# Sparse expert layer on one core: layer two in one PSUM group with one z operation, last scaling on VectorE, weight halves in a tile per chunk, no engine loop

## What is computed

```python
# x: (4096, 128) after the first layer norm; E = 8 experts, F = 512
router_probs = softmax(x @ Wr + br)
gates = max(router_probs); idx = argmax(router_probs)
xn = (x - mean) * rsqrt(var + 1e-5) * ln_g + ln_b
h = relu(xn @ W1[idx] + b1[idx])        # layer one
y = (h @ W2[idx] + b2[idx]) * gates     # layer two
out = layernorm(x + y)
```

## Time and profile before

| | |
|---|---|
| median of 3 runs | 221.95 us (221.65 to 223.75) |
| span of the profiled execution | 219.4 us |
| PE busy | 151.0 us (69%) |
| DVE busy | 171.0 us (78%) |
| ACT busy | 141.9 us (65%) |
| POOL busy | 122.4 us (56%) |

### The profile page before, as it was taken

One profiled execution on the slowest core, in us unless ns is written; L12 is line 12 of the kernel. 1 busy time (PEld: TensorE's weight loads), 2 busy tenths in 40 slices (PEclk: granted clock), 3 DMA queues, 4 the chain that ended last, 5 costly groups with the idle time before them and its releaser, 6 DMA issues.

```text
span 219.4 us, 5683 instructions
## 1 busy us (share of the span) xinstructions
PE 151.0 (69%) x1395; PEld 125.6 (57%) x1396; DVE 171.0 (78%) x792; ACT 141.9 (65%) x425; POOL 122.4 (56%) x210
## 2 busy tenths in 40 slices
PE   0158975989785989662500199979979979979600
PEld 0014854776664768552400089869869869868500
DVE  2538789878889889986779139989979979989910
ACT  2455619473817386658502288979979979989530
POOL 4322233325728676687777220667767767768670
PEclk9999997585968596655555559999999999999955
DMA  5996760000101010100133211222221221220000
GB/s 154 334 366 190 224 185 0 3 1 0 51 0 38 17 37 14 51 25 25 37 93 106 75 37 28 65 62 56 71 73 52 64 73 54 70 62 23 30 9 0
DMA packets 16409, 15.66 MB, mean 71 GB/s; under 512 B 2810, under 2 KB 13142, under 8 KB 16386
## 3 DMA queue, kind: packets, MB, share of 16 engines
q1 hardware_dynamic: 13458, 10.83, 17.4%
q0 software_dynamic: 2272, 4.27, 5.9%
q10 hardware_dynamic: 656, 0.30, 0.5%
HBM read 10.52 MB, written 5.33 MB: 72 GB/s over the span
## 4 chain that ended last, share of the span: by engine, by line
PE 37%; POOL 18%; issue 13%; DVE 12%; ACT 8%; DMA 5%; DVEq 2%; SPq 1%; ACTq 1%; POOLq 1%
POOL rows L374 12%; PE bank L559 7%; PE bank L545 4%; PE bank L547 4%; PE bank L549 4%; PE bank L548 4%; PE bank L562 3%; PE bank L450 3%; DMA XN<-in_attn_embeddings 3%; PE bank L471 3%; PE bank L518 2%; POOL rstd L362 2%; POOL R L366 2%; ACT sq L578 2%; DVE hl L1006 2%
## 5 line engine op out<-in xcount | busy, mean ns | idle before, releaser
L405 POOL DMA_INDIRECT out<-OUT,tok x39 | 40.5, 1038 | 29.3 <-issue 29.0
L374 POOL DMA_INDIRECT rows<-R,place x32 | 33.9, 1061 | 9.0 <-issue 9.0
L545 PE MATMUL bank<-sel,bias 96*128 (+1 forms) x156 | 35.2, 225 | 5.2 <-issue 5.2
L547 PE MATMUL bank<-xh,W1h 128*128 128x128 f16 x156 | 35.0, 225 | 0.0
L549 PE MATMUL bank<-xh,W1l 128*128 128x128 f16 x156 | 34.8, 223 | 0.0
L548 PE MATMUL bank<-xl,W1h 128*128 128x128 f16 x156 | 34.7, 222 | 0.0
L559 PE MATMUL bank<-W2hl,hh 128*128 x156 | 32.7, 274 | 0.9 <-DVE hl L1006 0.8
L1006 DVE SCALAR_TENSOR_TENSOR hl<-bank,hh 128x512 f16<-128x512 f32 x39 | 26.6, 682 | 6.5 <-ACT hh L682 6.4
L450 PEld LDWEIGHTS bank<-V,C 128*128 128x128 f32 x128 | 24.9, 299 | 11.2 <-issue 11.2
L450 PE MATMUL bank<-V,C 128*128 128x129 f32 x128 | 26.8, 393 | 3.0 <-DVE Y L772 3.0
L562 PE MATMUL bank<-W2hl,hl 128*128 x156 | 28.0, 219 | 0.0
(11 more groups left out here) (162 smaller groups left out, 448.8 us busy)
## 6 DMA issues: line engine op xcount, KB each, us to landing
XR<-rows SPq DMA_DIRECT2D x39, 66.0 KB, 1.8
W<-in_ffn_W SPq DMA_DIRECT2D x1, 2048.0 KB, 11.5
X<-in_attn_embeddings SPq DMA_DIRECT2D x2, 512.0 KB, 9.0
X<-in_attn_embeddings SPq DMA_DIRECT2D x1, 768.0 KB
out<-OUT,tok POOLq DMA_INDIRECT x39, 2.3
XN<-in_attn_embeddings SPq DMA_DIRECT2D x2, 256.0 KB, 8.3
rows<-R,place POOLq DMA_INDIRECT x32, 2.4
C<-in_constants SPq DMA_DIRECT2D x1, 428.0 KB, 4.6
```

What stands on the lines that cost most here:

```text
L374: pool.indirect_dma_start(out=rows[:, :], out_offset=bass.IndirectOffsetOnAxis(ap=place[u % 4][:, k:k + 1], axis=0), in_=R[u % 4][:, k, :] ...
L405: pool.indirect_dma_start(out=out[:, :], out_offset=bass.IndirectOffsetOnAxis(ap=tok[k][:, 0:1], axis=0), in_=OUT[k][:, :], in_offset=None ...
L545: pe.matmul(h, bias3[:, c * P:(c + 1) * P], sel, start=True, stop=False)
L547: pe.matmul(h, wh, xh[k][:, :], start=False, stop=False)
```

## The change

1. Layer two: the weight halves lie in separate tiles, and all products go to the same 128 columns. Per block there are 13 products of 128 columns in place of 4 of 256 and 5 of 128: the same number of columns, four more instructions with four more weight loads. One `z` operation on DVE takes the place of `z0` and `z`.
2. The last scaling moves: `fin` is now a `tensor_scalar` on DVE (subtract the mean, multiply by rec), and `shift` is gone. ACT has no `fin`. `sd` on ACT goes from lead -2 to lead -1, and `fin` on DVE has lead -2.
3. The weight halves are cut by chunks of 128 hidden units, over all experts, in place of pairs of experts; each operation has as many elements as before.
4. There is no engine loop: all 39 blocks are written out. PE and SP load the registers for the next 8 blocks in the middle of the 8 before.

```diff
-            steps(pe, [(1, b_h), (4, b_xT), (0, b_y)], load_experts)
+            def b_next(count, k):
+                if k == UN // 2 and (count(0) + 1) * UN < NB:
+                    load_experts((count(0) + 1) * UN)
...
-                for c in range(FC):
-                    w = W2hl[:, bass.ds(e * FC + c, 1), :]
-                    pe.matmul(y[:, 0:2 * D], hh[k][:, c * P:(c + 1) * P], w, start=c == 0, stop=False)
...
+                pe.matmul(y[:, 0:D], sel16[:, count(0) * UN + k:count(0) * UN + k + 1].to_broadcast([96, P]), bias3[:, FF:FF + D], start=True, stop=False)
                 for c in range(FC):
+                    wh, wl = W2h[c][:, bass.ds(e, 1), :], W2l[c][:, bass.ds(e, 1), :]
+                    pe.matmul(y[:, 0:D], hh[k][:, c * P:(c + 1) * P], wh, start=False, stop=False)
+                    pe.matmul(y[:, 0:D], hl[k][:, c * P:(c + 1) * P], wh, start=False, stop=False)
+                    m = pe.matmul(y[:, 0:D], hh[k][:, c * P:(c + 1) * P], wl, start=False, stop=c == FC - 1)
                 m.then_inc(every["y_ps"], 1)
...
+            steps([(1, b_h), (4, b_xT), (0, b_next), (0, b_y)])
...
-            steps(act, [(5, b_xs), (1, b_hh), (-3, b_fin), (4, b_xt), (-2, b_sd), (4, b_xh)])
+            steps([(5, b_xs), (1, b_hh), (4, b_xt), (-1, b_sd), (4, b_xh)])
...
-            def b_shift(count, k):
+            def b_fin(count, k):
+                after(dve, stored[k], count(0) * 16)
                 dve.wait_ge(every["rec"], blocks(count(0), k))
...
+                ts(OUT[k][:, :], z[k][:, :], mv2[k][:, 0:1], sd[k][:, 1:2], ALU.subtract, ALU.mult).then_inc(every["out"], 1)
...
-            steps(dve, [(1, b_hl), (-1, b_mv), (0, b_z0), (-2, b_rec), (0, b_z), (-2, b_shift), (0, b_bn), (4, b_xl)])
+            steps([(1, b_hl), (-1, b_mv), (-2, b_rec), (0, b_z), (-2, b_fin), (0, b_bn), (4, b_xl)])
```

More of the change, by code:

```diff
@@ L180, in build @@
         mv2 = [sb(f"mv2{i}", [P, 2]) for i in range(UN)]
-        sd = [sb(f"sd{i}", [P, 3]) for i in range(UN)]
+        sd = [sb(f"sd{i}", [P, 2]) for i in range(UN)]
         OUT = [sb(f"OUT{i}", [P, D]) for i in range(UN)]
@@ L193, in build @@
         padded = sem("padded")
-        names2 = "xs xh xl hl z".split()
+        names2 = "xs xh xl hl".split()
         t = {n: [sem(f"b_{n}{i}") for i in range(UN)] for n in names2}
-        every = {n: sem("every_" + n) for n in "token xT_ps xt h_ps hh y_ps z0 bn mv sd rec shift out".split()}
+        every = {n: sem("every_" + n) for n in "token xT_ps xt h_ps hh y_ps z bn mv sd rec out".split()}
         seen = sem("seen")
@@ L222, in build @@
         LO_AT = (7, 9)
-        AHEAD = 1
         def after(eng, signal, count):
@@ L228, in after, with steps @@
                 eng.wait_ge(signal, count)
-        def steps(eng, stages, turn_starts=None):
+        def steps(stages):
             hi = max(lead for lead, _ in stages)
             lo = min(lead for lead, _ in stages)
[L235 to L257, removed]
+            for b in range(-hi, NB - lo):
+                for lead, f in stages:
+                    if 0 <= b + lead < NB:
+                        f(lambda d, turn=(b + lead) // UN: turn + d, (b + lead) % UN)
         def blocks(turn, k):
@@ L309, in _ @@
                 sp.wait_ge(scattered[i], 16 * NT * (NU // 4))
-            held_row = [sp.alloc_register(f"row{i}") for i in range(UN)]
+            held_row = [sp.alloc_register(f"row{i}") for i in range(2 * UN)]
             row = {}
             def load_rows(first):
-                n = min(UN, NB - first) if isinstance(first, int) else UN
-                sp.load(held_row[0:n], blk_row[0:1, bass.ds(first, n)])
+                n, half = min(UN, NB - first), first // UN % 2 * UN
+                sp.load(held_row[half:half + n], blk_row[0:1, first:first + n])
                 for j in range(n):
-                    row[j] = sp.snap(held_row[j], min_val=0, max_val=PADROW)
+                    row[first + j] = sp.snap(held_row[half + j], min_val=0, max_val=PADROW)
             def load(count, k):
-                after(sp, every["z0"], blocks(count(-1), k))
+                after(sp, every["z"], blocks(count(-1), k))
                 after(sp, every["token"], blocks(count(-1), k))
-                sp.dma_start(XR[k][:, :], rows[bass.ds(row[k], P), :]).then_inc(row_loaded[k], 16)
-            steps(sp, [(0, load)], load_rows)
+                sp.dma_start(XR[k][:, :], rows[bass.ds(row[count(0) * UN + k], P), :]).then_inc(row_loaded[k], 16)
+            load_rows(0)
+            for b in range(NB):
+                if b % UN == UN // 2 and b + UN // 2 < NB:
+                    load_rows(b + UN // 2)
+                load(lambda d, turn=b // UN: turn + d, b % UN)
             for k in range(UN):
@@ L407, in store @@
                     in_=OUT[k][:, :], in_offset=None, bounds_check=T - 1, oob_is_err=False).then_inc(stored[k], 16)
-            steps(pool, [(-3, store), (3, token)])
+            steps([(-3, store), (3, token)])
         @block.tensor
@@ L993, in _ @@
             dve.drain().then_inc(s["table"], 1)
-            for q in range(len(LO_AT), E // 2):
-                split_lo(q)
+            for c in range(len(LO_AT), FC):
+                split_lo(c)
             dve.drain().then_inc(s["split_lo"], 1)
```

67 lines of the change are left out of this document (23 added, 44 removed).

## The result

The changed kernel takes 227.59 us (median of 4 runs, 227.46 to 227.65), the kernel before in the same set 222.85 us (4 runs, 221.65 to 224.04). The ratio is 1.020, with a 95% interval of 1.015 to 1.026: slower, by 4.7 us. The prediction said 224.0, with a range of 222 to 228. The profiled executions have spans of 225.8 and 219.4 us, 6.4 apart; they are one execution each, the medians are 4.7 apart.

The account below looks back on a forecast made before the run. ACT and DVE were taken to bound the kernel at 1.88 us a block, a circle between them afterwards at 2.12. +2.5 - 0.8 + 0.3 = +2.0 us on 221.95 gave 224.0 us; own range 222.4 to 226.3, with rivals 222.0 to 228.0.

Parts of the forecast that it names:

- slow rivals: The slower alternatives to the forecast, together 0.14: PE as bound (10%), OUT on DVE held by stores (3%), falling clock (1%).
- the 1% line: The time of 224.2 us, above which the change counts as slower by over 1%; the forecast's 78% was split about it.
- What bounds the kernel before: Second stage: ACT and DVE set the pace together at 1.88 us a block, with PE close behind at 1.75.
- The circle: ACT and DVE wait for each other, hh, hl, mv, sd, xh, xs, hh: 2.12 us a step, +2.5 us in all.
- the leaks: Register loads on PE between transpose and layer two delay later blocks by 0 to 0.3 us each: +0.3 us of 0 to 1.2.
- PE's cost: Layer two on PE takes 0.9 us, between 0.72 and 0.98, making PE's step 1.93, under 2.12.
- Nothing on the path: PE's step of 1.93 us is under the 2.12 of the ACT-DVE loop, so it adds no time.
- PE becomes the bound: Rival, 10%: layer one's 8 register operations on PE show too, step 2.27 us, time 229.4 us.
- DVE's own work: DVE's work without zpart's and shift's slots but with OUT: about 1.83 us a step.
- The end: From hh of the last block to the last store: 6.7 us in place of 7.47, -0.8 us.
- The loop: Engine loop's PE stalls, 5.2 us: by the rows 4.1 are register loads that stay; removal saves at most 5.2.
- OUT held by the stores: Rival, 3%: OUT on DVE waits up to 1.05 us for POOL's stores; step up to 2.8, time up to 248 us.

## Why the prediction was right, and where it was off

**The number.** The change was forecast at +2.0 us and came out at +4.7. The mechanism was right; 227.59 is above the forecast's own range (222.4 to 226.3) and lies within 222 to 228, a range set wider for its slow rivals. None of these happened; that 227.59 still fell inside is in part luck. The terms that were too small are named below. The chances hold a slip: a forecast "split evenly" about the 1% line gives 0.39 above it, not 0.34.

**What bounds the kernel before: right.** ACT and DVE set 1.88 together, and the run with mv ahead of hl in the kernel without the loop shows that relieving DVE alone gains nothing.

**The circle: right in place, short in size.** It went through the named instructions, with the named idle ahead of sd (0.57) and hl (0.46). At 2.19 it was outside the stated 2.08 to 2.17, and the 36 steps grew by 5.75 us, where the prediction had +2.5 for the circle (at most +4.3) and +0.3 for the leaks. The 2.9 us between are:

- 31 regular steps of 2.19 in place of 2.12: +2.1. The step that failed is "hh start to hl start: 0.63", taken from a row of before; it is 0.68 to 0.70. The prediction allowed 0.01 to 0.02 for a start after a wait, but the second wait is an instruction of its own and costs 0.06 to 0.07. The row was taken inside the engine loop, where the trace has no such instruction. Outside the loop, as in all of the changed kernel, the same trace shows 133.28 - 132.57 = 0.71:

```profile
133.28 0.69 DVE L1006 SCALAR_TENSOR_TENSOR hl<-bank,hh 128x512 f16<-128x512 f32 x1
```

- the last four steps, 1.90 each (204.34 to 211.93) and not 1.73: +0.7. In the first two there is no xs, and the circle still sets the step, 2.19 less 0.30. In the last two, with neither xh nor xs (1.63 predicted), hh waits for PE's layer two and layer one, which hold the step at 1.90. The first two:

```profile
206.23 0.58 ACT L661 ACTIVATE hh<-bank 128x512 f16<-128x512 f32 x1
...
207.72 0.29 ACT L665 ACTIVATE sd<-mv,epsc 128x1 f32<-128x1 f32 x1 [0.56 <-DVE mv L992]
```

- the fourth register load, 2.62 in place of a step of 2.12 and 0.3 of leak: +0.2. The first three leaked next to nothing. The prediction took each load at 0.87, from loads of nine numbers; with eight they take 0.60, and only the last took 1.07:

```profile
L509 PEldq TENSOR_LOAD <-blk_e x5: 592/605/1075, 122.5 to 192.0; - x5
```


**PE's cost: a term in order, a conclusion that was not.** Layer two was taken at 0.9 of 0.72 to 0.98 and is 0.97; PE's step was taken at 1.93 and is 1.96 with the scatters away. "Nothing on the path" held for the changed kernel. But the forecast counted PE only up to its own work; with the register loads and the late starts of hh it was 2.16 in the run with the square root late, almost the circle. The rival "PE becomes the bound" (2.27) was not what happened: layer one and the transpose took 1.02 with layer two's register operations left out, so layer one's own stayed hidden. Yet it named the engine of the second bound, which is why undoing the circle alone gained nothing.

**DVE's own work.** Predicted 1.83; it is 2.19 - 0.46 = 1.73 (the slot of OUT is 164.33 - 164.07 = 0.26, where the prediction added 0.28 of 0.24 to 0.28; the slot of rec fell from 0.12 to 0.05, 163.78 to 163.83; and the 1.91 that it started from was the step after a stall, where the regular one is 1.88). With the second z operation back (0.24) it is 1.96, as measured.

**The end: right.** -0.8 predicted, -0.7 found; the last store at 218.77 is 6.84 us after the last hh, with 6.7 predicted.

**The loop.** The prediction said that of the 5.2 us of stalls most were register loads, which stay. The Trainium skill, Runtime: NRT & Kernel Launch, section Instruction fetch mechanics, puts a fetch on a taken branch whose target is not in the window. The trace agrees that the loop has a price, but no run here shows a fetch. Without the loop 3.4 us were gained, and with the loads hidden too 5.0; in the 36 steps it was 2.5 us (72.24 to 69.74) and 2.4 more (to 67.34). So both shares are there, about equal: more was the loop's, and less the loads', than the 1.1 and 4.1 of the prediction. In the changed kernel none of this showed, under the circle.

**OUT held by the stores: did not happen.** For most blocks OUT starts just before a scatter's end (164.07, scatter 163.09 to 164.14) and takes 0.34 us. In the last blocks it runs wholly inside one (209.80, scatter 209.16 to 210.21) and takes 0.39 to 0.47, longer than before, but the next operation starts 0.25 later as always. The Trainium skill, SBUF — State Buffer, section Who interferes with whom, has the loser of the shared port pair blocked fully when a VectorE instruction runs in a two-port mode; this trace does not show a full block of OUT.

## What to carry to other kernels

When an instruction is moved one block earlier, follow its operand back on the other engine's own order: if the producer stands behind something that this engine makes in the same step, the two run in a circle, whose length is a sum of starts and not the work of either. Try the cheap cure first, the producer's place in its engine's order. And when undoing one suspect gains nothing, undo both before clearing either: two bounds at 2.19 and 2.16 hid each other here.

## What the runs showed of the hardware

- In half of the traces TensorE's signals come late beside GpSimd's scatters, in the others not at all. With the square root late, 44 of 47 signals that fell 0.6 to 1.2 us after the start of a 1.05 us scatter were late, and hh began up to 0.75 us later than the usual 0.10 after its product. In the changed kernel's trace none of 53 was late. The cause is not known; a comparison between traces must look for it first.
- Two register operations of 32 ns a chunk were not hidden in the new layer two, with three products of 128 columns a chunk: 0.22 us and not 0.17 with fixed addresses. The old layer two, with its wide products and one register operation a chunk, took 0.72 us in all, the new one 0.97, and 0.74 with fixed addresses.
- A second wait on one DVE instruction is an instruction of its own in code without an engine loop, 21 ns long, and adds 0.06 to 0.07 us between a signal and the start.
